# Thin-head attention with its value products gathered from two key blocks, a full last feed-forward block, and stored parts without repetition

## The chip, the cores and the metric

The kernel runs on one core of one Trainium2 chip. The time is the device time of one execution in microseconds. Three executions of the kernel before took 7369.84 to 7376.01 us, median 7372.24 us.

## What is computed

The reference is a stack of four layers on 4096 rows of 256 features. Each layer is an attention-like part and a feed-forward-like part, and each part ends in a residual addition and a layer norm:

```
x = _layernorm(x + _L0_attn_ref(...))   # 16 heads of 16 features, causal, rotary
x = _layernorm(x + _L0_ffn_ref(...))    # two local transformers; each ends in a gated feed-forward, 682 hidden
x = _layernorm(x + _L1_attn_ref(...))   # 16 heads of 16, relative-position bias, not causal
x = _layernorm(x + _L1_ffn_ref(...))    # projection with quantised operands
x = ...                                 # L2: state scan, experts; L3: recurrence
x = _layernorm(x + _L3_ffn_ref(...))    # two local transformers again
```

The change touches the two thin-head attentions (L0 and L1), the four gated feed-forwards, and the output projection of the L1 attention.

## The kernel before, in words

The stack is a sequence of stages with a barrier between them. The names of tiles begin with the stage: Aqkv, Aatt, Aout for the L0 attention; B0ffn and B1ffn, later H0ffn and H1ffn, for the gated feed-forwards; Cqkv, Catt, Cout for the L1 attention; Dmx is the stage after it.

**Products for the heads (`stage_qkv`, L584 to L733).** There are 8 chunks of 512 rows (B = 4 batches, two halves). In a chunk TensorE makes four product blocks (Q and K, two halves of the features each) and then four blocks of V. VectorE turns each Q or K block into an f32 tile, casts it to bf16 (the first of three parts) and subtracts (`split_high`, L660); GpSimd makes the second and third part. ScalarE's queue issues the stores. Q and K are stored as a stack of six terms in `q_parts` and `k_parts`, in which parts are repeated (Q: 0,1,2,0,1,0; K: 0,0,0,1,1,2), so that a score is a sum over 96 rows. The tile of parts and the tile of V have two buffers each; a buffer is free again when its stores have landed (`o_out`, `vo_out`).

**Thin attention (`stage_thin_attention`, L1077 to L1460).** Work goes over 8 pairs of heads times 4 batches; this gives 32 rounds of 16 steps. The order on each engine is written out by `written_out` (L101): at step i TensorE runs `scores` of step i (1024 keys for 128 queries; causal: only those up to the query), `turn_maxima`, `scores_by_key` of unit i-26 (two halves of 512 queries, called c = 0 and 1) and `values` of unit i-29. VectorE runs `add_near` of unit i-26 (Catt alone: it adds the near part of the bias to the queries close to the key block), and then `mask` of step i, which also takes the row maximum. ScalarE runs the exponentials of unit i-26, c = 0 before c = 1, and further on `move_out`, which copies the finished output of a round. Unit i of a round is head i % 2 of key block i // 2; the `values` call of unit i multiplies V with the half c = i % 2 of both heads of its key block, on four strips of 32 columns of the array.

The scores of a step have a ring of two buffers (`s_ps`), so that `scores` of step i waits for `mask` of step i-2. The products by key have a ring of two banks in Catt and three in Aatt (`T_R`), so in Catt a half c of a unit waits for the exponential of the same half of the unit before it. The output has one bank in Aatt, two in Catt (`O_R`). The exponentials' tile holds four key blocks (`NB`).

**Gated feed-forward (`stage_gated_ffn`, L1697).** The hidden 682 features are 5 blocks of 128 and one of 42. `down` (L1868) accumulates for each 128 rows the products of the six blocks (L1876). An f32 matmul is two instructions in the trace.

**Output projection (`stage_thin_out`, `Tail`).** `Tail` adds the residual, normalises and stores the result by rows; it also transposes it on TensorE (`turn`, L253), copies it on ScalarE and stores it by columns.

Of the kernel before, what the change touches and what calls it, by code (L numbers as in the profile page):

```python
# [16 lines left out]
ALU = mybir.AluOpType  # L17
# [9 lines left out]
B = 4  # L27
# [14 lines left out]
Q_STACK = ((0, 3, 0), (3, 2, 0), (5, 1, 0))  # L42
K_STACK = ((0, 3, 0), (3, 2, 1), (5, 1, 2))
# [99 lines left out]
class Tail:  # L143
# [4 lines left out]
    def __init__(self, nc, pl, out, res, base=None, bias=None, norm=True, y_ring=2, t_ring=2, tp=None, final=None):  # L148
        self.nc, self.pl, self.out, self.res, self.base, self.bias, self.norm = nc, pl, out, res, base, bias, norm
        self.y_ring, self.t_ring, self.final = y_ring, t_ring, final  # L150
# [18 lines left out]
        if final is None:  # L169
# [32 lines left out]
    def combine(self, v, it, u):  # L202
# [27 lines left out]
        for g in range(LN):  # L230
            m = u - (LN - 1) + g
            if self.final is None:
                v.wait_ge(self.t_done, it * NT + (m + 1))
# [9 lines left out]
    def prime_pe(self, t):  # L243
        t.sem_inc(self.y_done, NT)
        t.wait_ge(self.ident_made, 1)
        if self.final is None:
            t.sem_inc(self.t_done, LN)
# [5 lines left out]
    def turn(self, t, it, u):  # L253
        if self.final is not None:
            return
# [9 lines left out]
    def prime_act(self, s):  # L265
        if self.final is None:
# [3 lines left out]
        for i in range(IN if self.final is None else 0):  # L270
            s.sem_inc(self.cols_out[i], 16)

    def store(self, s, it, u):
# [5 lines left out]
        s.dma_start(rows_of(self.out, it, u * P, P), self.xn[:, g, :]).then_inc(self.rows_out[g], 16)  # L279
        s.wait_ge(self.t_done, n + 1 + LN)  # L280
# [6 lines left out]
    def finish(self, s):  # L287
# [3 lines left out]
        for i in range(IN if self.final is None else 0):  # L291
# [292 lines left out]
def stage_qkv(nc, name, act_in, wq, wk, wv, wqs, wks, bias, rope, q_s, k_s, v_s, scale):  # L584
# [5 lines left out]
    with ExitStack() as ctx:  # L590
# [16 lines left out]
        o_out = [pl.sem(f"o_out{i}") for i in range(2)]  # L607
# [52 lines left out]
        def split_high(v, s, it, c, j):  # L660

            v.drain()
            v.wait_ge(o_out[s], it * 192 + (c * 2 + j // 2 + 1) * 48)
            v.tensor_copy(parts[:, s, 0, :], o_sb[:, s, :])
            v.drain()
            v.tensor_tensor(rest[:, s, :], o_sb[:, s, :], parts[:, s, 0, :], ALU.subtract).then_inc(o_high, 1)

        @block.gpsimd
        def _(g):
            g.sem_inc(o_used, 2)  # L670
            with g.Fori(0, B) as it:
                for i in range(8):
# [3 lines left out]
                    g.tensor_copy(parts[:, s, 1, :], rest[:, s, :])  # L676
                    g.drain()
                    g.tensor_tensor(parts[:, s, 2, :], rest[:, s, :], parts[:, s, 1, :], ALU.subtract).then_inc(o_used, 1)
# [3 lines left out]
        def _(v):  # L682
# [3 lines left out]
            for it in range(B):  # L686
                for c in range(2):
# [16 lines left out]
                    for u in range(4):  # L704
                        s, n = u % 2, it * NT + (c * 4 + u)
                        v.wait_ge(v_done, n + 1 + NT)
                        v.wait_ge(vo_out[s], it * 64 + (c * 2 + u // 2 + 1) * 16)
                        if roped:
                            v.tensor_tensor(vo[:, s, :], v_ps[s][:], brow[:], ALU.add).then_inc(vo_done, 1)
# [2403 lines left out]
```

## Time and profile before

| | us |
|---|---|
| median of three executions | 7372.24 |
| profiled execution, its own time | 7380.4 |
| its span, first to last instruction | 7378.7 |
| TensorE busy | 6109.4 (83%) |
| VectorE busy | 4644.4 (63%) |
| ScalarE busy | 2720.1 (37%) |
| GpSimd busy | 1321.6 (18%) |
| mean granted TensorE clock | 0.921 of full |

The profile is one execution. Busy shares are averages over many stages with different limits, so each stage is read in its own stretch of time: Aqkv begins at 98.6 us, Aatt has its first score at 306.0 us, Cqkv begins at 2703.6 us, Catt has its first score at 2885.8 us, and Cout runs until about 3955 us.

### The profile page before, as it was taken

What the parts mean: (1) busy time and instruction counts of PE and PEld (TensorE: products, weight loads), DVE (VectorE), ACT (ScalarE), POOL (GpSimd) and SP (SyncE); (2) the same over time, 40 slices, a digit from 0 to 9 for tenths busy, and PEclk for the clock granted to TensorE, in tenths of its full rate; (3) what the DMA queues carried; (4) which work ended last, traced back from release to release, by engine and by line L of the source; (5) the groups of instructions that cost most, each with busy time, mean ns of one, the idle gap of its engine ahead of it and who ended that gap; (6) DMA issues with size and microseconds to landing.
All of it is one profiled execution on the core that took longest, in us unless ns stands there. A gap on an engine that the chain in (4) does not pass through costs nothing. (4 is left out here: it accounts for less than half of the span.)

```text
span 7378.7 us, 109245 instructions
## 1 busy us (share of the span) xinstructions
PE 6109.4 (83%) x31152; PEld 3249.8 (44%) x31152; DVE 4644.4 (63%) x11759; ACT 2720.1 (37%) x6050; POOL 1321.6 (18%) x1051
## 2 busy tenths in 40 slices
PE   5788859989988976999974488987996888998989
PEld 2333334655456542222223353334554456444755
DVE  4666648634764546999967648984435775347735
ACT  0155514722364211666651115541110354224711
POOL 1211107100431012000000005540002431015100
PEclk9899979989999987999997799988998999999989
DMA  5433244662456435323314221124222456224641
GB/s 163 134 70 72 64 126 146 199 201 72 133 177 203 136 109 161 89 73 88 87 48 117 82 75 48 37 61 112 69 67 86 133 168 216 73 90 152 195 147 54
DMA packets 946481, 836.62 MB, mean 113 GB/s; under 512 B 240872, under 2 KB 801984, under 8 KB 945728
## 3 DMA queue, kind: packets, MB, share of 16 engines
q1 hardware_dynamic: 498352, 507.29, 23.9%
q10 hardware_dynamic: 425472, 304.20, 13.3%
q0 software_dynamic: 22144, 18.99, 0.8%
q8 instruction: 236, 3.87, 0.2%
q14 instruction: 277, 2.27, 0.1%
HBM read 506.25 MB, written 346.03 MB: 116 GB/s over the span
## 5 line engine op out<-in xcount | busy, mean ns | idle before, releaser
L1414 ACT ACTIVATE Catt_E<-Catt_t 128x512 f32<-128x512 f32 x1024 | 579.2, 596 | 320.5 <-DVE Catt_t L1377 242.1
L1363 DVE CUSTOM_DVE_ANT_0 Catt_S<-Catt_s,Catt_win 128x1024 f32<-128x1024 f32 x512 | 621.5, 1215 | 5.8 <-DMA Catt_win<-skewed 3.9
L1363 DVE CUSTOM_DVE_ANT_0 Aatt_S<-Aatt_s,Aatt_win 128x128 f32<-128x128 f32 (+7 forms) x512 | 379.1, 757 | 227.9 <-PE Aatt_s L1290 201.1
L1414 ACT ACTIVATE Aatt_E<-Aatt_t 128x512 f32<-128x512 f32 (+3 forms) x768 | 341.4, 491 | 244.8 <-PE Aatt_t L1322 199.0
L1319 PE MATMUL Catt_t<-Catt_Q,Catt_K 123*128 123x512 bf16 x1024 | 363.8, 387 | 48.2 <-ACT Catt_E L1414 20.9
L1290 PE MATMUL Catt_s<-Catt_K,Catt_Q 96*128 96x512 bf16 x1024 | 321.9, 397 | 23.3 <-DMA Catt_K<-k_parts 12.3
L1377 DVE TENSOR_TENSOR Catt_t<-Catt_t,Catt_near 128x256 f32<-128x256 f32 (+2 forms) x640 | 284.7, 457 | 85.2 <-PE Catt_t L1319 77.1
L1341 PE MATMUL Catt_o<-Catt_E,Catt_V 128*32 128x256 f32 x4096 | 326.5, 391 | 0.0
L2381 PE MATMUL scan_cum<-scan_X,scan_upto 128*128 128x512 f32 x512 | 265.4, 608 | 25.8 <-DVE scan_X L2450 24.0
L2379 PE MATMUL scan_cum<-scan_X,scan_after 128*128 128x512 f32 x448 | 239.6, 617 | 40.8 <-DVE scan_pi L2461 40.8
L1341 PE MATMUL Aatt_o<-Aatt_E,Aatt_V 128*32 128x256 f32 (+1 forms) x2816 | 220.7, 358 | 41.6 <-ACT Aatt_O L1422 41.6
L1290 PE MATMUL Aatt_s<-Aatt_K,Aatt_Q 96*128 96x512 bf16 (+3 forms) x768 | 220.0, 343 | 38.2 <-DVE Aatt_nmax L1363 26.7
L1319 PEld LDWEIGHTS Catt_t<-Catt_Q,Catt_K 123*128 123x128 bf16 x1024 | 96.2, 96 | 342.7 <-ACT Catt_E L1414 297.4
L1319 PE MATMUL Aatt_t<-Aatt_Q,Aatt_K 99*128 99x512 bf16 (+3 forms) x768 | 232.2, 333 | 14.9 <-ACT Aatt_turned L1404 11.5
L2648 ACT ACTIVATE moe_sg<-moe_g 128x512 f32<-128x512 f32 x80 | 47.8, 597 | 361.4 <-PE moe_u L2591 361.4
L2381 PEld LDWEIGHTS scan_cum<-scan_X,scan_upto 128*128 128x128 f32 x512 | 99.6, 196 | 155.7 <-issue 155.7
L1290 PEld LDWEIGHTS Catt_s<-Catt_K,Catt_Q 96*128 96x128 bf16 x1024 | 58.9, 98 | 245.8 <-DVE Catt_nmax L1363 118.6
L2591 PE MATMUL moe_g<-moe_xc,moe_wg 128*128 128x512 f32 x320 | 154.8, 607 | 11.9 <-DVE moe_hid L2724 11.6
L2362 POOL TENSOR_TENSOR scan_pr<-scan_pr,scan_pi 128x1024 f32<-128x1024 f32 x64 | 150.9, 2358 | 42.4 <-DVE scan_pr L2461 42.4
L2379 PEld LDWEIGHTS scan_cum<-scan_X,scan_after 128*128 128x128 f32 x448 | 83.4, 195 | 166.2 <-issue 166.2
L2355 POOL TENSOR_TENSOR scan_X<-scan_cs,scan_r 128x1024 f32<-128x1024 f32 x64 | 121.7, 1902 | 188.8 <-DVE scan_X L2450 188.8
L2167 PE MATMUL state_in_z<-state_in_wj,state_in_xc 128*128 128x288 f32 x512 | 140.8, 431 | 15.9 <-DVE state_in_wj L2192 15.9
(723 smaller groups left out, 14037.1 us busy)
## 6 DMA issues: line engine op xcount, KB each, us to landing
moe_cb<-c_s SPq DMA_DIRECT2D x16, 1024.0 KB
skewed<-lines POOLq DMA_DIRECT2D x8, 1920.0 KB, 12.8
Catt_win<-skewed SPq DMA_DIRECT2D x16, 960.0 KB, 4.8
rec<-state_in_r ACTq DMA_DIRECT2D x32, 416.0 KB
scan_r<-rec SPq DMA_DIRECT2D x64, 208.0 KB, 2.5
Aatt_Q<-q_parts SPq DMA_DIRECT2D x32, 384.0 KB, 4.2
Aatt_K<-k_parts SPq DMA_DIRECT2D x32, 384.0 KB, 5.5
Catt_Q<-q_parts SPq DMA_DIRECT2D x32, 384.0 KB, 4.3
```

The costliest lines, as they stand in the source:

```text
L1290: ins = t.matmul(s_ps[j % 2][:, c:d], Q[0:K0, b, h, u * P:(u + 1) * P], K[0:K0, b, h, c:d], start=True, stop=True)
L1319: ins = t.matmul(bank(it, n)[:, 0:hi - lo], K[:, b, h, kb * P:(kb + 1) * P], Q[:, b, h, lo:hi], start=True, stop=not diagonal)
L1341: ins = t.matmul(o_ps[b % O_R][f:f + 2 * hd, k0 * P:k1 * P], V[:, b, kb, h, :], blocks[:, h, x, k0:k1, :], start=kb == 0 and c == 0, stop= ...
L1363: v.tensor_tensor_reduce(out=S[:, j % 2, 0:w], in0=s_ps[j % 2][:, 0:w], in1=win[:, 0 if causal else h, w0:w0 + w], scale=-1.0, scalar=BIG, ...
L1377: v.tensor_tensor(x, x, near[:, b, h, a - (kb - 1) * P:z - (kb - 1) * P], ALU.add).then_inc(near_done, 1)
L1414: a.activation(E[:, kb % NB, h, lo:hi], bank(it, n)[:, 0:hi - lo], ACT.Exp, scale=scale).then_inc(exped, 1)
L2167: t.matmul(z_ps[s][:], xc[:, c, kt, q * P + j + 1:q * P + j + 1 + P], wj[:, kt, j, :], start=j == 0 and kt == 0, stop=j == TAPS - 1 and kt ...
L2355: g.tensor_tensor(X[:, m % 4, 0, :].rearrange("p (k e) -> p k e", k=16), cs[:, m % 2, :].rearrange("p (k e) -> p k e", k=16), r[:, m % R, ...
L2362: g.tensor_tensor(pr[:, m % 2, :], pr[:, m % 2, :], pi[:, m % 2, :], ALU.add).then_inc(sum_done, 1)
L2379: t.matmul(cum[i][:, c:c + 512], after[:], X[:, (j - 1) % 4, i, c:c + 512], start=False, stop=False, skip_group_check=True)
L2381: ins = t.matmul(cum[i][:, c:c + 512], upto[:], X[:, j % 4, i, c:c + 512], start=u == 0, stop=True, skip_group_check=True)
L2591: ins = t.matmul(ps[k % 2][:], w[:, kt, j * P:(j + 1) * P], xc[:, c, kt, :], start=kt == 0, stop=kt == KT - 1)
```

## The change

The diff has five parts.

1. In both thin attentions the value products are no longer made at each step. They are made for four units (two key blocks) in a row, at the step at which the last of them was made before.
2. `q_parts` and `k_parts` hold each of the three parts once, not six terms. Each product block is stored by three DMAs of one part each; the loads of the attention make the stack: three DMAs for Q and six for K in place of one and one. The tile of parts has four buffers, and V has one per half; a chunk's V is stored by one DMA in place of four.
3. In the gated feed-forward the last block is used in full: rows 42 to 127 of `hid` and `w2_sb` are set to zero once by GpSimd, and the product goes over 128 rows.
4. The Cout stage no longer makes the transposed result (`cols=False`): no transposes, no ScalarE copies, no stores by columns.
5. Waits are counted to match; VectorE waits for the zeroed tails once, and the sync queue before its last weight load.

```diff
-Q_STACK = ((0, 3, 0), (3, 2, 0), (5, 1, 0))
-K_STACK = ((0, 3, 0), (3, 2, 1), (5, 1, 2))
+STACK = ((0, 3, 0), (3, 2, 1), (5, 1, 2))
...
     def turn(self, t, it, u):
-        if self.final is not None:
+        if not self.cols:
             return
...
         s.dma_start(rows_of(self.out, it, u * P, P), self.xn[:, g, :]).then_inc(self.rows_out[g], 16)
+        if not self.cols:
+            return
...
+        PR = 4
-        parts = pl.sb("parts", [P, 2, PARTS, CH], BF16)
+        parts = pl.sb("parts", [P, PR, PARTS, CH], BF16)
-        vo = pl.sb("vo", [P, 2, C])
+        vo = pl.sb("vo", [P, 2, 4, C])
...
-            v.wait_ge(o_out[s], it * 192 + (c * 2 + j // 2 + 1) * 48)
-            v.tensor_copy(parts[:, s, 0, :], o_sb[:, s, :])
+            v.wait_ge(o_out[j], it * (32 * PARTS) + (c + 1) * (16 * PARTS))
+            v.tensor_copy(parts[:, j, 0, :], o_sb[:, s, :])
...
-                        v.wait_ge(vo_out[s], it * 64 + (c * 2 + u // 2 + 1) * 16)
+                        if u == 0:
+                            v.wait_ge(vo_out[c], it * 16 + 16)
...
-                        for t0, nt, part in K_STACK if w else Q_STACK:
-                            a.dma_start((k_s if w else q_s)[m * P:(m + 1) * P, t0:t0 + nt, bass.ds(it * T + c * CH, CH)],
-                                        parts[:, s, part:part + 1, :].to_broadcast([P, nt, CH]) if w else
-                                        parts[:, s, part:part + nt, :]).then_inc(o_out[s], 16)
-                    for u in range(4):
-                        s, n = u % 2, it * NT + (c * 4 + u)
-                        a.wait_ge(vo_done, n + 3)
-                        a.dma_start(v_s[bass.ds(it * T + (c * CH + u * P), P), 0:C], vo[:, s, :]).then_inc(vo_out[s], 16)
+                        rows = (k_s if w else q_s).rearrange("(e k f) t -> e k f t", k=PARTS, f=16)[m * 8:(m + 1) * 8, :, :, bass.ds(it * T + c * CH, CH)]
+                        for k in range(PARTS):
+                            a.dma_start(rows[:, k], parts[:, j, k, :]).then_inc(o_out[j], 16)
+                    a.wait_ge(vo_done, it * NT + (c * 4 + 6))
+                    a.dma_start(v_s[bass.ds(it * T + c * CH, CH), 0:C].rearrange("(q p) d -> p q d", p=P), vo[:, c]).then_inc(vo_out[c], 16)
...
-                for x, x_s in ((Q, q_s), (K, k_s)):
-                    sp.dma_start(x[0:K0, b], x_s.rearrange("f t c -> (f t) c")[bass.ds(it * (2 * K0), 2 * K0), b * T:(b + 1) * T]
-                                 .rearrange("(h p) c -> p h c", h=2)).then_inc(head_in[b], 16)
+                for t0, nt, part in STACK:
+                    rows = slice(t0 * hd, (t0 + nt) * hd)
+                    sp.dma_start(Q[rows, b], head_rows(q_s, it, b)[:, 0:nt * hd].rearrange("h p c -> p h c")).then_inc(head_in[b], 16)
+                    for h in range(2):
+                        sp.dma_start(K[rows, b, h], head_rows(k_s, it, b)[h:h + 1, part * hd:(part + 1) * hd].to_broadcast([nt, hd, T])
+                                     ).then_inc(head_in[b], 16)
...
-            written_out(t, PAIRS, ST, ((0, scores), (TURN, turn_maxima), (LAG, scores_by_key), (LAG + 3, values)))
+            def values_of_two_blocks(it, i):
+
+                if i % 4 == 3:
+                    for k in range(i - 3, i + 1):
+                        values(it, k)
+
+            written_out(t, PAIRS, ST, ((0, scores), (TURN, turn_maxima), (LAG, scores_by_key), (LAG + 3, values_of_two_blocks)))
...
+            g.memset(hid[:, :, NJ - 1, :], 0.0).then_inc(tails_zero, 1)
+            g.memset(w2_sb[:, NJ - 1, :], 0.0).then_inc(tails_zero, 1)
...
-                        ins = t.matmul(tail.y[u % 2][:], hid[0:M[j], c, j, (u % 4) * P:(u % 4 + 1) * P], w2_sb[0:M[j], j, :],
+                        ins = t.matmul(tail.y[u % 2][:], hid[:, c, j, (u % 4) * P:(u % 4 + 1) * P], w2_sb[:, j, :],
...
-    stage_thin_out(nc, "Cout", oT_s, i["L1_wo"], nxt, cur)
+    stage_thin_out(nc, "Cout", oT_s, i["L1_wo"], nxt, cur, cols=False)
```

## Rows read from the trace of the kernel before

**Rows 1.** Windows: stretch, its us, busy of each engine, granted clock, DMA share, GB/s.

```profile
338.00:922.00 584.00, 512.38 (x4592) 200.93 (x4591) 363.42 (x989) 343.33 (x780) 61.64 (x149) 0.99 0.30 67
1600.00:1868.00 268.00, 264.06 (x849) 145.97 (x848) 103.44 (x306) 65.28 (x136) 8.61 (x8) 0.99 0.32 95
2707.00:2876.00 169.00, 109.24 (x253) 59.82 (x251) 76.50 (x127) 0.00 (x0) 57.04 (x64) 0.81 0.58 191
2932.00:3792.00 860.00, 820.50 (x5796) 222.97 (x5799) 803.42 (x1592) 563.82 (x1021) 61.87 (x149) 1.00 0.31 78
```

**Rows 2.** Lines by form, Catt on VectorE: busy, mean ns | idle before, releasers.

```profile
L1363 DVE CUSTOM_DVE_ANT_0 Catt_S<-Catt_s,Catt_win 128x1024 f32<-128x1024 f32 x512 | 621.5, 1215 | 5.8 <-DMA Catt_win<-skewed 3.9 <-issue 0.5
L1377 DVE TENSOR_TENSOR Catt_t<-Catt_t,Catt_near 128x384 f32<-128x384 f32 x256 | 145.1, 567 | 55.8 <-PE Catt_t L1319 52.3
L1377 DVE TENSOR_TENSOR Catt_t<-Catt_t,Catt_near 128x256 f32<-128x256 f32 x256 | 110.1, 430 | 19.0 <-PE Catt_t L1319 15.3
```

**Rows 3.** Source line L1363 from 3000 to 3700 us: min/median/max ns, first and last start.

```profile
L1363 DVE CUSTOM_DVE_ANT_0 Catt_S<-Catt_s,Catt_win x391: 1210/1215/1225, 3000.5 to 3699.3; 128x1024 f32<-128x1024 f32 x196
```

**Rows 4.** Timeline of TensorE in Catt: start, us, instruction, count.

```profile
3351.71 0.64 PE L1341 MATMUL Catt_o<-Catt_E,Catt_V 128*32 128x256 f32 x8
3352.28 0.60 PE L1290 MATMUL Catt_s<-Catt_K,Catt_Q 96*128 96x512 bf16 x2
3352.73 0.60 PE L1319 MATMUL Catt_t<-Catt_Q,Catt_K 123*128 123x512 bf16 x2
3353.26 0.64 PE L1341 MATMUL Catt_o<-Catt_E,Catt_V 128*32 128x256 f32 x8
```

**Rows 5.** Timeline of VectorE and ScalarE in Catt, single rows.

```profile
3356.65 0.57 DVE L1377 TENSOR_TENSOR Catt_t<-Catt_t,Catt_near 128x384 f32<-128x384 f32 x1 [0.25 <-PE Catt_t L1319]
...
3358.33 0.57 DVE L1377 TENSOR_TENSOR Catt_t<-Catt_t,Catt_near 128x384 f32<-128x384 f32 x1
...
3357.25 1.08 ACT L1414 ACTIVATE Catt_E<-Catt_t 128x512 f32<-128x512 f32 x2 [0.86 <-DVE Catt_t L1377]
```

**Rows 6.** Timeline of TensorE at the end of Catt: four units in a row.

```profile
3838.38 1.93 PE L1341 MATMUL Catt_o<-Catt_E,Catt_V 128*32 128x256 f32 x32
```

**Rows 7.** Timeline in B0ffn: the products of `down`, and the weight loads of the short block.

```profile
1625.20 11.89 PE L1876 MATMUL B0ffn_y<-B0ffn_w,B0ffn_hid 128*128 128x256 f32 x48
...
1627.45 0.29 PEld L1876 LDWEIGHTS B0ffn_y<-B0ffn_w,B0ffn_hid 42*128 42x128 f32 x2 [0.33 <-issue]
```

**Rows 8.** Aatt: the masks of all rounds (tile Aatt_s), and TensorE's timeline.

```profile
L1363 DVE CUSTOM_DVE_ANT_0 Aatt_S<-Aatt_s,Aatt_win x512: 285/756/1226, 309.3 to 923.5; 128x768 f32<-128x768 f32 x22, 128x128 f32<-128x128 f32 x22, 128x512 f32<-128x512 f32 x22, 128x640 f32<-128x640 f32 x21
...
610.63 0.64 PE L1341 MATMUL Aatt_o<-Aatt_E,Aatt_V 128*32 128x256 f32 x8 [1.34 <-ACT Aatt_O L1422]
```

**Rows 9.** Waits in Cqkv (us, times, longest), and one chunk's end in the timeline.

```profile
DVE Cqkv_vo L711 <- DMA v_s<-Cqkv_vo: 59.6, 12, 8.7
DVE Cqkv_parts L664 <- DMA q_parts<-Cqkv_parts: 27.6, 15, 3.5
...
2763.86 3.78 PE L656 MATMUL Cqkv_v<-Cqkv_w_v,Cqkv_hT 128*128 128x256 f32 x8 [6.23 <-DVE Cqkv_vo L711]
2767.44 3.65 PE L650 MATMUL Cqkv_a<-Cqkv_hT,Cqkv_w_q 128*128 128x512 f32 x8
...
2772.51 0.68 DVE L693 TENSOR_SCALAR Cqkv_o<-Cqkv_a 128x512 f32<-128x512 f32 x1
```

**Rows 10.** The same place in Aqkv.

```profile
126.11 1.88 PE L650 MATMUL Aqkv_b<-Aqkv_hT,Aqkv_w_qs 128*128 128x512 f32 x4
...
128.36 0.74 DVE L697 SCALAR_TENSOR_TENSOR Aqkv_tmp<-Aqkv_a,Aqkv_bcol,Aqkv_cos 128x512 f32<-128x512 f32 x1
```

**Rows 11.** Timeline of VectorE in Cout: a wait for TensorE.

```profile
3877.57 0.42 DVE L208 TENSOR_TENSOR Cout_z<-Cout_y,Cout_res 128x256 f32<-128x256 f32 x1 [0.41 <-PE Cout_y L1502]
```

**Rows 12.** DMA: ScalarE's queue from 2707 to 2876 us; a load, median us to landing.

```profile
q10 hardware_dynamic: 30432, 29.11, 51.5%
...
Catt_K<-k_parts SPq DMA_DIRECT2D x31, 384.0 KB, 5.7
```

More of the change, by code:

```diff
@@ L143, with __init__ @@
 class Tail:
-    def __init__(self, nc, pl, out, res, base=None, bias=None, norm=True, y_ring=2, t_ring=2, tp=None, final=None):
+    def __init__(self, nc, pl, out, res, base=None, bias=None, norm=True, y_ring=2, t_ring=2, tp=None, final=None, cols=True):
         self.nc, self.pl, self.out, self.res, self.base, self.bias, self.norm = nc, pl, out, res, base, bias, norm
-        self.y_ring, self.t_ring, self.final = y_ring, t_ring, final
+        self.y_ring, self.t_ring, self.final, self.cols = y_ring, t_ring, final, cols and final is None
         self.y = [pl.ps(f"y{i}", (P, C)) for i in range(y_ring)]
@@ L269, in prime_act @@
             s.sem_inc(self.rows_out[i], 16)
-        for i in range(IN if self.final is None else 0):
+        for i in range(IN if self.cols else 0):
             s.sem_inc(self.cols_out[i], 16)
@@ L290, in finish @@
             s.wait_ge(self.rows_out[i], 16 + 16 * B * NT // LN)
-        for i in range(IN if self.final is None else 0):
+        for i in range(IN if self.cols else 0):
             s.wait_ge(self.cols_out[i], 16 + 16 * B * NT // IN)
@@ L662, in split_high @@
             v.drain()
-            v.wait_ge(o_out[s], it * 192 + (c * 2 + j // 2 + 1) * 48)
-            v.tensor_copy(parts[:, s, 0, :], o_sb[:, s, :])
+            v.wait_ge(o_out[j], it * (32 * PARTS) + (c + 1) * (16 * PARTS))
+            v.tensor_copy(parts[:, j, 0, :], o_sb[:, s, :])
             v.drain()
-            v.tensor_tensor(rest[:, s, :], o_sb[:, s, :], parts[:, s, 0, :], ALU.subtract).then_inc(o_high, 1)
+            v.tensor_tensor(rest[:, s, :], o_sb[:, s, :], parts[:, j, 0, :], ALU.subtract).then_inc(o_high, 1)
         @block.gpsimd
@@ L675, in _ @@
                     apart(g, pl.pool_unread)
-                    g.tensor_copy(parts[:, s, 1, :], rest[:, s, :])
+                    g.tensor_copy(parts[:, i % PR, 1, :], rest[:, s, :])
                     g.drain()
-                    g.tensor_tensor(parts[:, s, 2, :], rest[:, s, :], parts[:, s, 1, :], ALU.subtract).then_inc(o_used, 1)
+                    g.tensor_tensor(parts[:, i % PR, 2, :], rest[:, s, :], parts[:, i % PR, 1, :], ALU.subtract).then_inc(o_used, 1)
                     g.drain()
@@ L1460, in _, with stage_thin_out @@
                 a.wait_ge(o_out[i], 64 + 64 * PAIRS)
-def stage_thin_out(nc, name, oT_s, w, out, res, bias=None):
+def stage_thin_out(nc, name, oT_s, w, out, res, bias=None, cols=True):
     with ExitStack() as ctx:
         pl = Pool_(nc, ctx, name)
-        tail = Tail(nc, pl, out, res, None, bias, True)
+        tail = Tail(nc, pl, out, res, None, bias, True, cols=cols)
         w_sb = pl.sb("w", [P, KT, C])
@@ L1719, in stage_gated_ffn @@
         a_ps = [pl.ps(f"a{i}") for i in range(2)]
-        small_in, wl_zero, w1_in, w2_in = (pl.sem(n) for n in ("small_in", "wl_zero", "w1_in", "w2_in"))
+        small_in, wl_zero, w1_in, w2_in, tails_zero = (pl.sem(n) for n in ("small_in", "wl_zero", "w1_in", "w2_in", "tails_zero"))
         hs_in = [pl.sem(f"hs_in{i}") for i in range(LN)]
@@ L1827, in _ @@
             v.wait_ge(small_in, 64)
+            v.wait_ge(tails_zero, 2)
             batches(v, batch)
```

32 lines of the change are left out of this document (18 added, 14 removed).

## The prediction

> **What bounds the kernel now.** I read the windows by stage first, because the page's mean (TensorE 83% busy) mixes stages with different limits. Then came, for each stage that the change touches, the lines, the waits and the timeline of the engine that is never idle there.
>
> Catt: TensorE is busy 820 of 860 us and VectorE 803 of 860 [rows 1]; both look full. The timeline separates them. A step of TensorE is products by key to values 0.53 us, values to scores 0.57, scores to products by key 0.45, together 1.55 us [rows 4]. VectorE needs 1.68 us for a step with a near part of 384 queries (start to start in [rows 5]), and by the mean durations [rows 2] 1.54 with 256 and 1.82 where the near part falls in both halves. Of a round's 16 units 4 have 256, 8 have 384 and 4 have both: 4 x 1.54 + 8 x 1.68 + 4 x 1.82 = 26.9 us. The round really takes 16 x (3699.3 - 3000.5)/390 = 28.7 us [rows 3]. So VectorE bounds Catt, and 1.8 us a round are its waits for products by key [rows 2, 5]. Aatt has no near part; VectorE is busy 62%, TensorE 88% [rows 1], and a round takes 16 x (923.5 - 309.3)/511 = 19.2 us [rows 8]: TensorE bounds it. In the feed-forward TensorE is busy 264 of 268 us [rows 1]. In Cqkv VectorE stands 59.6 + 27.6 = 87 of 169 us before buffers whose stores have not landed [rows 9].
>
> **Feed-forward.** Four row blocks of 12 matmuls take 11.89 us [rows 7]. In an unbroken run such matmuls start every 0.22 us: 32 of them, four side by side, take 1.93 us, the last 0.38 of it [rows 6]. With 47 such intervals and the last matmul that is 10.3 + 0.4 = 10.7, so 1.2 us less; the rest sits at the loads of the 42-row block, each behind 0.33 us [rows 7], and the exit from the last block adds 0.1 to 0.2. I take 0.36 us a row block, 32 blocks, 4 stages: -46 us (bounds -38 and -52). All of it is on the path, since nothing else is as busy. The two memsets run beside the first weight loads; VectorE's wait stands ahead of its first gate, with the combines behind it, and the sync queue's ahead of the last weight load and the residual loads, none of which is wanted for tens of us. Uncovered they cost 1 to 2 us a stage.
>
> **Cqkv.** V now has a buffer for each of a chunk's four blocks, so the waits of 59.6 us go; the parts have four buffers, so the 27.6 us go. Late next is TensorE: the third and fourth V block start when VectorE has freed the first two (2763.86), and the next chunk's first Q block follows at 2767.44 and is ready half of 3.65 us later, 2769.3; VectorE began it at 2772.51 [rows 9]. That gives 3.2 us a chunk, and the parts another 2.5: 5.7 x 8 = -45 us. Bounds: -87 if all waits go, -10 if the longer store of V and GpSimd's parts, which VectorE must share time with, take their place. In Aqkv the same change meets a later TensorE: the second product of the next chunk ends at 126.11 + 1.88 = 127.99, and VectorE started at 128.36 [rows 10]. That is 0.4 x 8 = 3, with the end -4 us (0 to -20, if the clock stays high there).
>
> Here a rule of the Trainium skill bears on the cost. "DMA: Bandwidth & Descriptors", section "Why a DMA increments its semaphore by 16 and not by 1", says that a DMA is spread over the largest number up to 16 that divides both sides' slowest dimension. The new stores of parts have 8 there, so by it they use half the engines. No trace here shows it. In rows: ScalarE's queue took 51.5% of 16 x 169 us for 30432 packets, 0.046 us each [rows 12]. A chunk now has 12 stores of 128 packets, on 8 engines 12 x 16 x 0.046 = 8.8 us, and V 1.5, under a chunk of about 15 us. So by itself it does not bind, but it is the reason why I give the loss of this gain a chance.
>
> **Cout.** The transposes stand between TensorE's products; VectorE waits 0.41 us [rows 11] and some 0.2 more for them in each group of four row blocks. 0.6 x 8 and the last copy and store by columns: -6 us (0 to -10).
>
> **The loads.** Nine DMAs stand where two stood, 7 more at about 0.45 us of issue, 3 us a load, with V, tables, window and the round trip of the maxima queued behind them. A load starts when the round's values are done, 20 steps before its first score, 24 us in Aatt and 35 in Catt; before, it landed 5.7 us after issue [rows 12]. Hidden but for the first load of each stage: +5 us for both (0 to +10). Without that cover it would be 3 us a round.
>
> **Values in Catt.** A unit in a run costs 0.43 us (1.93 less 0.64, over three [rows 4, 6]), alone it costs 0.53 + 0.57 less 0.44 (products by key to scores directly): 0.66. Merging saves TensorE 0.23 x 12 = 2.8 us a round, but TensorE is not the bound. What counts is where the run stands. At every fourth step TensorE does: products by key of unit k, then 0.53, then the run of four until the next scores 0.57 + 1.29 = 1.86, then 0.45 of scores, and only then the products by key of unit k+1, 2.84 us after those of unit k. It cannot make them earlier: the engine works in order, and the ring of two banks makes them wait for the exponentials of unit k. VectorE's near part of unit k+1 waits for them, and the next mask is queued behind it, though its scores are there. Where the near part is in the first half, the second half of unit k is held back by its exponential: near part 0.57, two exponentials 1.08 [rows 5] and hand-over, 1.75 us after the near part of unit k-1 against a step of 1.68. With a product's 0.42 until VectorE may start, the run then begins 0.27 later: 3.1 us. So the round's four steps with a run cost 2 x 2.84 + 2 x 3.1 = 11.9 us. The other twelve go at VectorE's pace, since TensorE has 0.9 us of work in them: 3 x 1.54 + 6 x 1.68 + 3 x 1.82 = 20.2. With 0.4 for the turned maxima the round is 32.5 us instead of 28.7: +3.8 x 32 = **+122 us**. Bounds: +150 if all four steps lose another 0.2, and -75 if the order did not hold VectorE and its waits for products by key went altogether (55.8 + 19.0 [rows 2]); I take 122, because each of its terms is a row.
>
> **Values in Aatt.** 12 runs a round become 4, 8 x 0.2 = 1.6 us less. The first values of a round now come three steps later, and so the wait of 1.34 us for the one output bank [rows 8] goes, since ScalarE's copy has long been made. 2.9 us on offer. Against it: in the twelve steps without values TensorE runs into VectorE's masks (up to 1.2 us each for 1024 keys [rows 8]) and ScalarE's exponentials (two in 0.99, being 1.08 less 0.09 of hand-over [rows 5]). Walking the round with these, I lose half: -1.4 x 32 = -45 us (bounds 0 and -93). The exponentials' buffers are free in time: unit k waits for the values of unit k-8, made at least two steps before.
>
> **Sum.** -46 - 45 - 4 - 6 + 5 - 45 + 122 = -19 us. The profiled execution took 7380.4 (span 7378.7), 8 above the median; the sum holds for either: 7361 for such a profile, **7353 us** for the median. About 0.2%, 15 us, is what a measurement of this kernel tells from no change.
>
> **Rivals.**
> Runs do not stall VectorE in Catt, and its waits shrink. For it: TensorE is 95% busy there and VectorE does wait for it. Against: the order on both engines. Half to all of the 75 us gained instead of 122 lost: 7153 to 7195, say 7185.
> The granted clock falls in Catt. It is 1.00 at 95% busy, but 0.81 in Cqkv at 65% [rows 1]; with runs I expect (0.95 x 28.7 - 2.8)/32.5 = 75% busy. At 0.90, a fifth of the time at 1.2 GHz, a step with a run grows by some 2.4 us: 4 x 0.2 x 2.4 = 1.9 a round, +61: 7414, slower than before. Against: the gaps are 1.3 us at most, in Cqkv 6.23 [rows 9]. It decides the sign from about 0.94.
> The stores pay nothing in Cqkv (fewer engines, or GpSimd takes the waits over): +45, 7398, slower.
> The change does not do what it says, in that the 42-row block is no dearer than a full one: +46, 7399. The 0.33 us before its loads speak against it; I count it with the one before.
>
> **How the numbers follow.** Forecast 0.60, with its own range 7315 to 7390; first rival 0.14, second 0.13, third with fourth 0.13. The forecast's terms err by some 30 us together, mostly Catt and Aatt, so within it faster, same, slower are 0.58, 0.28, 0.14. That gives faster 0.35 + 0.14 + 0.01 = 0.50, slower 0.08 + 0.12 + 0.09 = 0.29, the same 0.21. The range leaves out most of the first rival and little above: 7265 to 7420.
>
> **What would show it.** In Catt, four steps of a round at 2.8 to 3.1 us between masks, the idle time of L1377 before products by key up from 75 to about 200 us, TensorE's share down, clock still 1.00. In Aatt no wait for the output copy and rounds near 17.8 us. In the feed-forward 48 matmuls in 10.6 us. In Cqkv chunks of 15 us and no DMA wait. Wrong it would be if Catt's rounds stayed under 29 us, or if its clock fell.

## The result, and the profile after

The kernel after takes 7492.72 us (median of 4 runs, 7483.19 to 7503.07), the kernel before beside it 7374.12 (7369.84 to 7385.87): ratio 1.0159, 95% interval 1.014 to 1.0177, 119 us slower where 19 us faster was forecast, and outside the range. The profiled execution is the shortest of the four, 7483.19 us with a span of 7481.5, 103 above the span of before; the stages below add up to that.

From the end of the stage before to its own end, each stage changed by (us, after less before; a stage ends with the last operation of TensorE, VectorE or ScalarE on its tiles): Aqkv -12.9, Aatt +4.2, the four feed-forwards -10.6, -12.3, -12.5, -12.9, Cqkv -38.0, Catt **+193.6**, Cout -5.0, the stage behind it -2.4; the others, whose code is the same, together +12 (in the traces of the experiments these lie between -3 and +15, so that is scatter). One stage turns the sign.

The windows of the kernel after, in the order of [rows 1] (us, busy of PE, PEld, DVE, ACT, POOL, granted clock, DMA share, GB/s):

```profile
325.00:912.00 587.00, 498.26 (x4606) 227.33 (x4604) 355.56 (x996) 339.79 (x786) 61.66 (x149) 0.98 0.29 67
1582.00:1849.00 267.00, 252.18 (x855) 151.97 (x856) 108.44 (x330) 67.37 (x141) 8.63 (x8) 0.97 0.34 103
2680.00:2809.00 129.00, 100.72 (x248) 57.37 (x246) 84.61 (x124) 0.00 (x0) 57.80 (x64) 0.82 0.48 148
2860.00:3922.00 1062.00, 858.39 (x5908) 287.36 (x5908) 828.70 (x1634) 569.16 (x1052) 62.81 (x153) 0.94 0.24 64
```

In Catt TensorE and VectorE were 95% and 93% busy; now they are 81% and 78% busy. Neither is full, so they wait for each other. VectorE's lines there, as [rows 2], and its masks over the same part of the stage as [rows 3]:

```profile
L1377 DVE CUSTOM_DVE_ANT_0 Catt_S<-Catt_s,Catt_win 128x1024 f32<-128x1024 f32 x493 | 598.3, 1214 | 0.5
L1391 DVE TENSOR_TENSOR Catt_t<-Catt_t,Catt_near 128x384 f32<-128x384 f32 x248 | 140.5, 566 | 127.6 <-PE Catt_t L1327 127.6
L1391 DVE TENSOR_TENSOR Catt_t<-Catt_t,Catt_near 128x256 f32<-128x256 f32 x246 | 105.9, 430 | 101.4 <-PE Catt_t L1327 99.6
```

```profile
L1377 DVE CUSTOM_DVE_ANT_0 Catt_S<-Catt_s,Catt_win x376: 1211/1214/1225, 3001.1 to 3799.7; 128x1024 f32<-128x1024 f32 x188
```

The operations cost what they did. The idle time before the near parts went from 75 to 229 us, and a round takes 16 x 798.6/375 = 34.1 us. Where a round loses it is seen in TensorE's and ScalarE's timelines, as [rows 4, 5]:

```profile
3244.58 1.93 PE L1349 MATMUL Catt_o<-Catt_E,Catt_V 128*32 128x256 f32 x32
3246.45 0.60 PE L1298 MATMUL Catt_s<-Catt_K,Catt_Q 96*128 96x512 bf16 x2
...
3248.56 0.88 PE L1327 MATMUL Catt_t<-Catt_Q,Catt_K 123*128 123x512 bf16 x2 [0.64 <-ACT Catt_E L1428]
3249.28 0.60 PE L1298 MATMUL Catt_s<-Catt_K,Catt_Q 96*128 96x512 bf16 x2
3250.86 0.88 PE L1327 MATMUL Catt_t<-Catt_Q,Catt_K 123*128 123x512 bf16 x2 [0.99 <-ACT Catt_E L1428]
3251.58 0.87 PE L1298 MATMUL Catt_s<-Catt_K,Catt_Q 96*128 96x512 bf16 x2
3252.55 1.09 PE L1327 MATMUL Catt_t<-Catt_Q,Catt_K 123*128 123x512 bf16 x2
3253.57 2.70 PE L1349 MATMUL Catt_o<-Catt_E,Catt_V 128*32 128x256 f32 x32
...
3248.88 0.60 ACT L1436 ACTIVATE Catt_O<-Catt_o 128x512 f32<-128x512 f32 x1
3249.57 0.54 ACTq L1439 DMA_DIRECT2D Catt_sums<-Catt_O  x1
3250.21 1.09 ACT L1428 ACTIVATE Catt_E<-Catt_t 128x512 f32<-128x512 f32 x2 [0.73 <-DVE Catt_t L1391]
```

A run of 32 products takes 1.93 us, as in [rows 6]. Two gaps of TensorE follow the round's last run, with different causes. The first, 0.64 us, ends at 3248.56, before ScalarE begins its copy: it is the run's own, through VectorE's late near part and the exponential behind it. The second, 0.99 us, is that of exponentials that stand behind ScalarE's output copy and the issue of a DMA, 1.14 us together. Then the granted clock falls, and the next run takes 2.70. The same place in windows (their columns as above):

```profile
3238.30:3251.90 13.60, 10.51 (x70) 3.42 (x62) 10.31 (x22) 7.12 (x14) 1.27 (x1) 1.00 0.17 55
3251.90:3255.30 3.40, 3.31 (x24) 1.06 (x26) 2.95 (x6) 2.16 (x4) 0.83 (x4) 0.52 0.71 99
```

In Aatt [rows 8] the wait of 1.34 us for the output bank is gone, and this stands in its place in every round:

```profile
578.25 0.60 ACT L1436 ACTIVATE Aatt_O<-Aatt_o 128x512 f32<-128x512 f32 x1
...
578.93 0.54 ACTq L1439 DMA_DIRECT2D Aatt_sums<-Aatt_O  x1
...
579.58 1.81 ACT L1428 ACTIVATE Aatt_E<-Aatt_t 128x256 f32<-128x256 f32 x5 [0.73 <-ACT Aatt_O L1436]
...
580.02 0.39 PE L1327 MATMUL Aatt_t<-Aatt_Q,Aatt_K 99*128 99x512 bf16 x1 [1.26 <-ACT Aatt_E L1428]
```

Waits (us, times, longest) at the head of Catt, and in Cqkv, where [rows 9] had 59.6 and 27.6 us for DMAs and now no DMA stands among VectorE's waits. Of the 12.4 us for windows 3.8 lie ahead of the stage's first mask and 8.6 ahead of the ninth. Then the products of [rows 7], whose 48 starts now span 10.1 us:

```profile
PE Catt_s L1298 <- DMA Catt_K<-k_parts: 15.0, 1, 15.0
DVE Catt_S L1377 <- DMA Catt_win<-skewed: 12.4, 2, 8.6
...
DVE Cqkv_vo L714 <- PE Cqkv_v L658: 22.2, 15, 1.8
DVE Cqkv_o L695 <- PE Cqkv_a L652: 16.1, 7, 2.5
```

```profile
L1894 PE MATMUL B0ffn_y<-B0ffn_w,B0ffn_hid x48: 379/379/379, 1616.1 to 1626.2; 128*128 128x256 f32 x48
```

### The profile page after: what moved, and what is told of

It is laid out like the page before. It is cut to its first block and busy times, and to the rows that moved or that the text cites. A ratio compares the mean times of both kernels' runs of the same rounds, so it can differ in the third digit from the quotient of the medians.

```text
span 7481.5 us, 109988 instructions
## 1 busy us (share of the span) xinstructions
PE 6055.3 (81%) x31088; PEld 3357.7 (45%) x31088; DVE 4646.3 (62%) x11759; ACT 2688.4 (36%) x6018; POOL 1328.2 (18%) x1059
## 5 line engine op out<-in xcount | busy, mean ns | idle before, releaser
L1377 DVE CUSTOM_DVE_ANT_0 Catt_S<-Catt_s,Catt_win 128x1024 f32<-128x1024 f32 x512 | 620.8, 1214 | 14.0 <-DMA Catt_win<-skewed 12.4
L1327 PE MATMUL Catt_t<-Catt_Q,Catt_K 123*128 123x512 bf16 x1024 | 385.4, 406 | 184.5 <-ACT Catt_E L1428 147.4
L1349 PE MATMUL Catt_o<-Catt_E,Catt_V 128*32 128x256 f32 x4096 | 282.9, 423 | 0.0
L1349 PEld LDWEIGHTS Catt_o<-Catt_E,Catt_V 128*32 128x32 f32 x4096 | 130.1, 120 | 130.1 <-issue 68.8
L1349 PE MATMUL Aatt_o<-Aatt_E,Aatt_V 128*32 128x256 f32 (+1 forms) x2816 | 178.5, 367 | 0.0
L1281 POOL TENSOR_TENSOR Catt_O<-Catt_O,Catt_Rb 128x512 f32<-128x512 f32 x32 | 40.8, 1274 | 723.0 <-DMA Catt_Rb<-r_s 723.0
L1298 PEld LDWEIGHTS Catt_s<-Catt_K,Catt_Q 96*128 96x128 bf16 x1024 | 77.2, 99 | 197.4 <-DVE Catt_nmax L1377 110.2
```

The source lines that it names most:

```text
L1298: ins = t.matmul(s_ps[j % 2][:, c:d], Q[0:K0, b, h, u * P:(u + 1) * P], K[0:K0, b, h, c:d], start=True, stop=True)
L1327: ins = t.matmul(bank(it, n)[:, 0:hi - lo], K[:, b, h, kb * P:(kb + 1) * P], Q[:, b, h, lo:hi], start=True, stop=not diagonal)
L1349: ins = t.matmul(o_ps[b % O_R][f:f + 2 * hd, k0 * P:k1 * P], V[:, b, kb, h, :], blocks[:, h, x, k0:k1, :], start=kb == 0 and c == 0, stop= ...
L1377: v.tensor_tensor_reduce(out=S[:, j % 2, 0:w], in0=s_ps[j % 2][:, 0:w], in1=win[:, 0 if causal else h, w0:w0 + w], scale=-1.0, scalar=BIG, ...
```

## The experiments

The stages are apart from one another, so one kernel can carry an edit in each. Step k is the time from a round's mask k to the next mask; a round is 16 steps. This table is worked out from VectorE's timeline of each trace: mean rounds from the third on (us), medians of the steps that matter, and how often the granted clock falls from 2.4 to 1.2 GHz in the stage. Where the text speaks of rounds without a fall, they are counted from step 8 to step 8, since most falls lie near a round's end.

```
                 Catt round  steps 0 / 4 / 8 / 12 / 14 / 15          falls  Aatt round  falls
before             28.67     1.68  1.68  1.55  1.68  2.17  1.90         0     19.47       3
after              34.12     3.60  2.84  2.84  3.11  2.30  2.12        30     19.45       7
e1 step by step    28.73     1.68  1.68  1.55  1.68  2.17  1.90         0     19.58       5
e2 runs alone      34.14     3.61  2.84  2.84  3.11  2.30  2.12        31     19.54       8
e3 PE kept busy    34.21     2.95  2.84  2.84  3.54  2.30  1.90        12     18.25       0
e4 two units       30.68     2.09  1.97  1.97  2.24  2.30  1.90         2     18.63       0
e5 third bank      31.46     2.76  2.84  2.45  2.69  1.61  1.67        14     17.92       0
e6 first run only  27.32     2.76  1.61  1.47  1.61  1.61  1.67         0     18.13       0
e7 bank, loads     29.17     1.67  1.61  1.47  1.61  2.45  1.67        16     18.73       5
e8                 27.34     2.76  1.61  1.47  1.61  1.61  1.67         0     17.82       0
e9 shorter runs    28.18     1.67  1.61  1.47  1.61  1.61  3.02         7     18.59       2
e10 two banks      30.62     3.95  1.68  1.55  1.68  2.30  2.12        25     19.81       6
e11 issue later    34.07     2.95  4.38  2.84  3.11  1.68  1.90        28     18.76       0
```

**e1, step by step again in both attentions.**

```
-            written_out(t, ..., (LAG + 3, values_of_two_blocks)))
+            written_out(t, ..., (LAG + 3, values)))
```

> The kernel after, with the value products of both attentions issued step by step again; the other three parts of the change stay. Theory 1 (the runs of four are what costs: in Catt VectorE starves behind each run, in Aatt they are worth nearly nothing): Catt's rounds go back from 34.1 to 28.7 us, 31 x 5.4 = 170 us, Aatt's stay at 19.3; the whole is about 7295 us, 75 to 80 us below the kernel before. Theory 2 (the nine loads of parts per batch in place of two, and their 5 to 9 us of landing, hold up the rounds of Catt): rounds stay above 31 us and the whole above 7370.

Measured: 7312.38 us (7310.96 to 7314.04), 0.9908 of the kernel before (0.9891 to 0.9924). The runs are the whole loss; the rest of the change is worth 70 us. Catt, with the loads of the kernel after and rounds as before, is 10.0 us longer than in the kernel before: that is what the loads cost there. VectorE's waits for products by key fall back:

```profile
DVE Catt_t L1391 <- PE Catt_t L1327: 50.8, 143, 1.4
```

**e2, the runs alone on the kernel before.** The diff is `values_of_two_blocks` and its place in the order, nothing else.

> The kernel before with nothing changed but the value products in runs of two key blocks. Theory 1: Catt's rounds are 33.5 to 34.2 us as in the kernel after, so the whole is 160 to 180 us over the kernel before, 7535 to 7555 us, and Catt's first mask starts where it did. Theory 2 (the loads of parts and the runs cost together): rounds near 31 us, the whole under 7470.

Measured: 7562.05 us (7559.54 to 7571.73), 1.025 (1.0232 to 1.0267), +179. The same steps to 0.01 us, with two loads in place of nine: the loads have no part in the rounds.

```profile
DVE Catt_t L1383 <- PE Catt_t L1319: 210.8, 203, 2.8
```

**e3, three edits.**

```
+                again = 2 if not causal and j % GS in (13, 14, 15) else 1     # (a) scores
-                for c in range(0, w, CH):
+                for c in list(range(0, w, CH)) * again:
...
-            ..., (LAG + 4, move_out), ...        # (b) copy and issue of sums in one
+            ..., (LAG + 4, move_out), (LAG + (6 if causal else 4), gather_sums), ...
...
+                        rows = P if j < NJ - 1 else 64 if base is not None else 96     # (c)
-                        ... hid[:, c, j, ...], w2_sb[:, j, :], ...
+                        ... hid[0:rows, c, j, ...], w2_sb[0:rows, j, :], ...
```

> The kernel after with three separate edits. (a) Catt: the score products of steps 13 to 15 of each round are issued twice, 0.43 us each, in time in which TensorE now idles 1.0 to 1.4 us. If its idling there is what the granted clock answers to, the clock no longer falls at the run of step 0, step 0 goes from 3.6 to 3.1 us and the round from 34.1 to 33.5 (18 us in all); if the fall has another cause, the round stays or grows by up to 1.3 us. (b) Aatt: ScalarE's issue of the sums' DMA stands two steps behind the output copy instead of right behind it. If the 0.54 us of issue are the half of step 15 that matters, step 15 goes from 2.13 to about 1.6 us and the round from 19.05 to 18.5; if the copy alone sets it, nothing moves. (c) Feed-forward: the last hidden block of the down products has 96 rows in B0 and H0 and 64 in B1 and H1 instead of 128. If the 42-row block was dear because its weight load is not taken ahead at a size other than 128 rows, all four stages are 10 to 13 us longer than in the kernel after; if only sizes under some bound are dear, 96 rows cost nothing.

Measured: 7477.72 us (one run). (a) No fall at steps 14 and 15 any more (25 of 30 before), step 0 down from 3.60 to 2.95; but 8 of the 12 falls that are left are at step 3, and step 12 pays 0.43 us for the doubled scores. The mean round doesn't gain; the 17 rounds without a fall take 33.6 us. (b) Aatt's round falls by 1.2 us, and TensorE's wait ahead of its products by key from 1.26 to 0.43 us: the issue was in the way. Part of the 1.2 is the clock, which no longer falls; rounds without a fall went from 19.13 to 18.25. (c) The block of 96 rows runs like a full one (48 starts in 10.1 us), the one of 64 (11.6) like that of 42 in [rows 7] (11.5), with the same 0.33 us before its loads. That is the second reading, only sizes under some bound are dear; the bound lies between 64 and 96 rows.

```profile
L1901 PE MATMUL B0ffn_y<-B0ffn_w,B0ffn_hid x48: 377/379/381, 1587.7 to 1597.8; 128*128 128x256 f32 x40, 96*128 96x256 f32 x8
...
L1901 PE MATMUL B1ffn_y<-B1ffn_w,B1ffn_hid x48: 376/379/483, 2386.3 to 2397.9; 128*128 128x256 f32 x40, 64*128 64x256 f32 x8
...
2388.59 0.29 PEld L1901 LDWEIGHTS B1ffn_y<-B1ffn_w,B1ffn_hid 64*128 64x128 f32 x2 [0.33 <-issue]
```

**e4, runs of two units.** `if i % 2 == 1: for k in (i - 1, i)`; in Aatt `move_out` at LAG + 5. The condition on `i` holds in both attentions, so Aatt has runs of two as well, and not of four as the expectation says.

> The kernel after with (a) Catt: runs of two units (one key block, 16 products, 0.96 us) instead of four; Theory 1 (VectorE starves for what of a run does not fit under the bank that it has in hand): a run of two adds 0.2 to 0.5 us at eight steps, the round is 30 to 32 us, 34.1 with four and 28.7 with one; rival (any run costs a fixed stall of about 1.2 us, whatever its length, by a refilled pipeline or the clock): 8 x 1.2 more than 28.7, 38 us. (b) Aatt: runs of four as in the kernel after, but ScalarE's output copy and sums issue one step later. If the copy stands in the way because it waits for the last run, step 15 goes from 2.1 to below 1.7 us and the round to about 18.5; if it is the 1.14 us of ScalarE's own time, the loss moves one step on and the round stays at 19.05.

Measured: 7332.71 us, 0.9935 (0.9914 to 0.9955). Catt 30.68, as the theory of what doesn't fit under the bank in hand has it; a fixed stall per run is excluded. Its eight run steps take 1.83 to 2.30. Aatt tests nothing about the copy alone, since its runs are shorter too. Its steps 14 and 15 together take 3.93 us against 2.88 in the kernel after, and the wait for the output bank is back in every round; steps 0, 4 and 12 are shorter by 2.1, and the clock no longer falls:

```profile
575.77 1.07 PE L1349 MATMUL Aatt_o<-Aatt_E,Aatt_V 128*32 128x256 f32 x16 [1.35 <-ACT Aatt_O L1436]
```

**e5, a third bank for products by key in Catt.**

```
-        T_R, O_R = (3, 1) if causal else (2, 2)
+        T_R, O_R = 3, 1
```

In Aatt the output copy is `v.tensor_copy` on VectorE at LAG + 4, the sums' issue on ScalarE at LAG + 6; `window(0, 1)` stands behind `window(0, 0)`; the value blocks of `stage_qkv` are stored one by one.

> The kernel after with (a) Catt: three banks for the products by key and one for the values in place of two and two, the runs of four units kept. Theory 1 (with two banks VectorE has nothing in hand behind a run) says that a third lets it work on by one unit: the four run steps lose 0.5 to 1.1 us each and the round goes from 34.1 to 30 to 32 us. Rival (the run's 1.9 us of TensorE has to be paid anyway, because TensorE is busy 0.81 of the time and catches up late): the round stays above 33. The clock's falls at steps 14 and 15 stay in both. (b) Aatt: the copy of the output bank made by VectorE and the issue of the sums' DMA two steps later: if ScalarE's copy is worth anything beside the issue, the round goes below the 18.25 us that the later issue alone gave, to about 17.7; if not, it stays. (c) Cqkv: the value blocks are stored one by one as before, the parts unrepeated as after: if the stores of parts carry the gain, the stage is 145 to 148 us from end to end as in the kernel after; if the values' single store does, it is over 160. (d) The second window of Catt is loaded right behind the first: the 9.8 us in which VectorE waits for it in the first batch go.

Measured: 7318.46 us (one run). (a) 31.46, inside the forecast; but the gain isn't at all runs: step 4 is unchanged at 2.84 and 8 of 14 falls come just ahead of it. (b) 17.92. (c) Cqkv 145.1 us from end to end, 145.5 in the kernel after: the single store of V has no share in the gain. The eight V buffers stayed, so what they and the four buffers of parts each carry was not tried. (d) VectorE's waits for windows are gone; the second of them was 8.6 us.

**e6, only the first four units of a round in a run.**

```
-                if i % 4 == 3:
+                if i % GS >= 4:
+                    values(it, i)
+                elif i % GS == 3:
                     for k in range(i - 3, i + 1):
                         values(it, k)
```

with three banks and one in Catt, and the issue two steps later in Aatt.

> The kernel after with, in both attentions, a run only for the first four units of a round (so that the first value products come after the output bank is free) and the rest step by step; three banks for products by key and one for values in Catt; the issue of the sums' DMA two steps later in Aatt. Theory 1: a run costs where it stands, so Catt pays one and not four, 28.7 plus 0.5 to 1.3 us a round; Aatt keeps the relief at its bank and loses the stalls of steps 4 and 12, 17.6 to 18.0 us a round against 18.25. Whole: 7235 to 7285 us. Rival: the fourth run matters because the granted clock falls anywhere that TensorE idles, rounds of Catt over 31.

Measured: 7207.59 us, 0.9766 (0.9716 to 0.9816), below the forecast. Catt's round is 27.32 where 29.2 to 30 was expected, and its clock never falls. I had priced the run and not what the third bank gives to the other steps: 1.61 in place of 1.68, 1.61 and 1.67 at steps 14 and 15. The 26.9 us of the prediction is thus not VectorE's own pace. Its steps without a wait are 1.48 and 1.61 us here, 0.06 to 0.07 less than those that 26.9 was added up from; with them (4 x 1.48 + 8 x 1.61 + 3 x 1.67 + 1.81, the last four where the near part falls in both halves) I estimate VectorE's own round at 25.6.

```profile
L1379 DVE CUSTOM_DVE_ANT_0 Catt_S<-Catt_s,Catt_win x512: 1211/1215/1225, 2782.6 to 3653.6; 128x1024 f32<-128x1024 f32 x171
```

**e7, the third bank without any run in Catt; K's first loads on ScalarE.** Aatt as e6, issue at LAG + 7.

> The kernel after with (a) Catt step by step, three banks and one: if the depth of the ring limits Catt even without runs, its round goes below 28.7 (to 27.5), but the values must now wait for the single output bank, up to 1.2 us a round; my estimate is 28 to 29.5. (b) Aatt: first run only, the sums' DMA three steps later: 17.6 to 18.0 us a round as with two steps. (c) The first six loads of K parts of each attention are issued by ScalarE instead of SyncE, which takes 0.9 to 1.6 us over each pair, and the second window comes early: the first mask of Catt comes 3 to 6 us earlier, if issue and not the transfer is what it waits for. Whole: 7225 to 7270 us.

Measured: 7278.4 us, 0.9862 (0.9815 to 0.9908), 8 above the forecast's end. (a) 29.17: with a single output bank the values stand before ScalarE's copy every round, step 13 takes 3.67, and in 16 of the rounds the clock falls there. (c) A miss: the first mask comes 21.9 us after Cqkv's end, not sooner than 16.8. But ScalarE issued its six loads from 4.9 to 10.0 us after Cqkv's end, and SyncE's last load of K in the kernel after is issued by 9.8: the issue did not come earlier, and both windows and V were now loaded beside it. So what these loads wait for stays open.

```profile
PE Catt_o L1351 <- ACT Catt_O L1444: 63.7, 29, 2.2
```

```profile
PE Catt_s L1300 <- DMA Catt_K<-k_parts: 21.0, 1, 21.0
```

**e8, what the others point to:** e6 with e5's copy on VectorE and early window.

> First run only in both attentions, three banks and one in Catt (27.3 us a round so far), the second window early, and in Aatt VectorE's copy of the output bank with the sums' issue two steps later. If the gains in Aatt of the copy on VectorE (17.92 against 18.25 us with all runs) and of the first run only (18.13 with ScalarE's copy) are separate, Aatt's round is 17.3 to 17.8 us; Catt's stays at 27.3 and starts its rounds 8 us sooner after its first mask. Whole: 7180 to 7195 us. If the clock takes part of it back in Aatt (falls while TensorE waits), its round stays above 18.1.

Measured: 7191.21 us (7187.86 to 7192.77), **0.9734** of the kernel before (0.9721 to 0.9748), 194 us faster, and 301 below the kernel after. Both attentions run at a full clock:

```profile
330.00:850.00 520.00, 484.87 (x4454) 205.39 (x4453) 364.73 (x992) 315.37 (x733) 59.35 (x144) 1.00 0.32 75
2820.00:3630.00 810.00, 747.34 (x5708) 231.89 (x5707) 763.88 (x1570) 545.87 (x1006) 60.80 (x148) 1.00 0.32 83
```

The two gains in Aatt don't add up: 17.82 us against 17.92 with all four runs.

**e9, the run at the head shorter,** three units in Catt and two in Aatt.

> As the last, but the run at the head of a round has three units in Catt and two in Aatt. A run of four costs step 0 of Catt 2.76 us against 1.67; with three units TensorE's run is 0.5 us shorter and one step earlier. Theory 1: Catt's round falls by 0.3 to 0.6 us to 26.7 to 27.0, and Aatt's by 0 to 0.4. Rival: the output bank isn't free yet when the shorter run comes (ScalarE copies it in step 13 or 14), and the wait for it costs what the run gives back: Catt's round 27.3 or more, and with TensorE idle the clock falls.

Measured: 7239.56 us, 0.9801 (0.9783 to 0.9819). The rival: step 0 gives back 1.1 us, step 15 takes 1.35 more, and the clock falls 7 times. Of the lengths tried, four units is the one at which the output bank is free.

**e10, the single run with two banks and two in Catt;** in Aatt step by step, with the issue two steps later.

> (a) Catt: a run only for the first four units, with the banks as in the kernel after, two and two. It parts the third bank from the single run. Theory 1: 28.7 of the step-by-step order plus 1.2 to 1.9 us of the one run with its clock fall, 29.9 to 30.6 us a round; then the third bank is worth some 2.5 us a round beside it. Rival (the single run alone explains the 27.3 us): below 28.7. (b) Aatt: values step by step, with the sums' issue two steps later. The 1.3 us wait for the output bank stays and ScalarE's issue is hidden, as before: 19.2 to 19.4 us a round; if it falls towards 18.2, the issue was what cost before as well, and the runs nothing.

Measured: 7375.47 us (one run). Catt 30.62, so against e6 the third bank (with one for the values in place of two) is worth 3.3 us a round, 1.2 of it at step 0 (3.95 against 2.76), ahead of which the clock falls in 24 rounds here and in none of e6. The three rounds that no fall touches take 29.5, so some 2.2 us are the bank's own and the rest comes through the clock. Aatt 19.81: without runs the late issue is worth nothing, since the wait at the bank stays.

**e11, the sums' issue two steps later in Catt, the kernel after otherwise;** in Aatt the copy on VectorE, the issue right behind.

> The kernel after with (a) Catt: ScalarE's issue of the sums' DMA two steps behind its copy of the output bank instead of right behind it. In the kernel after the copy takes 0.60 us and the issue 0.54 us ahead of a unit's exponentials, steps 14 and 15 take 2.30 and 2.12 us, TensorE idles 0.64 and 0.99 us in them, and the granted clock falls in 25 of 30 cases in just these two. If the issue behind the copy is the cause of both, the two steps lose 0.3 to 0.6 us, the falls at steps 14 and 15 go, step 0 goes from 3.6 to 3.1, and the round from 34.1 to 33.0 to 33.4 us. If the copy or the bank of two is the cause, the round stays above 33.8. (b) Aatt: the copy is made by VectorE, with ScalarE's issue still right behind it in time, one step of the order later than the last run. If only the issue's place counts, ScalarE now waits for VectorE's copy as well and the round stays at 19 us or more; if ScalarE's 0.60 us for the copy count, it falls by up to 0.6.

Measured: 7444.8 us (one run). Steps 14 and 15 lose 0.84 us and step 0 loses 0.65, as the first theory says; the round stays at 34.07. Of the two gaps behind the last run the 0.64 us is still there, and the 0.99 has become 0.37. The fall of the clock has moved to step 3 in 25 of 28 cases, where TensorE waits for the turned maxima, and meets the run of step 4 instead:

```profile
3329.72 0.88 PE L1327 MATMUL Catt_t<-Catt_Q,Catt_K 123*128 123x512 bf16 x2 [0.64 <-ACT Catt_E L1436]
3331.40 0.88 PE L1327 MATMUL Catt_t<-Catt_Q,Catt_K 123*128 123x512 bf16 x2 [0.37 <-ACT Catt_E L1436]
...
3102.93 0.22 PE L1310 MATMUL Catt_t<-Catt_ident_b,Catt_parts 128*48 128x128 bf16 x1 [0.47 <-ACT Catt_E L1436]
3103.51 1.03 PE L1327 MATMUL Catt_t<-Catt_Q,Catt_K 123*128 123x512 bf16 x2 [0.36 <-ACT Catt_turned L1426]
3104.48 3.13 PE L1349 MATMUL Catt_o<-Catt_E,Catt_V 128*32 128x256 f32 x32
```

Without that fall the sum of its steps would be 34.07 - (4.38 - 2.84) = 32.5 us, and the two rounds without a fall take 32.5 and 32.9. The trace of the kernel after shows the same move by itself: in the five of its rounds that begin without a fall at steps 14 or 15 ahead of them, step 0 takes 2.9 us, and the clock falls at step 3 instead. In Aatt the copy's engine alone is worth 0.7 us a round, the issue's place alone 1.2 (e3), both 1.5 (e5); in all three the clock's 7 falls are gone too, which is part of it. Against the 19.13 us of the rounds without a fall in the kernel after, they are worth 0.4, 0.9 and 1.2.

## Why the prediction was wrong, by its own steps

The forecast was -19 us, the two traces differ by 103. Catt makes 69 of the difference (forecast +122 and half of +5, measured +193.6), Aatt 47 (-45 and the other half, measured +4.2), Cqkv 7.

**Values in Catt: the mechanism was right, the size was not.** The four steps were to take 2.84, 2.84 and twice 3.1; they take 2.84, 2.84, 3.11 and 3.60. Two terms of the walked round were mis-sized. "The other twelve go at VectorE's pace", 20.2 + 0.4: they take 34.0 - 12.4 = 21.6. The first is this one: the sum of VectorE's durations left out ScalarE's chain, its output copy and the issue behind it at steps 14 and 15, worth 0.84 us by e11. The second is the clock: I made it a rival of its own, at 0.90 and +61 us, instead of asking what the forecast's own gaps would do. A fall of the clock was one of the prediction's own signs of being wrong. It came to 0.94, where I had put the change of sign, but by itself it is only 29 x 0.65 = 19 us. Per round it is 0.65 us as it falls in the kernel after, and 1.5 us once the other loss is gone, so that taking away the 0.84 alone gained nothing. With neither, the round is the 32.5 us that the walk gave. The 1.68 us that the walk took for VectorE's own step holds with two banks only; e6 shows 1.61 with three, and what the other 0.07 are was not asked.

In numbers: 29 rounds x 5.45 = 158 us in place of 110, and 5 more in the last round; the drain from the last mask to VectorE's last operation 69.6 us in place of 49.0 (66.4 in e2, 49.0 in e1, so it is the runs'), which I hadn't priced: +21. The loads make the remaining 10. (A small slip beside it: the first rival's lower end adds up to 7156 us, not 7153.)

**The loads: +5 forecast, some +14 measured.** Entry of Aatt +3.9 us, of Catt +5.0 (first mask 16.8 us after Cqkv's end, was 11.7), and the second window, queued behind the eighteen loads of two batches, makes VectorE wait 8.6 us where it was 3.9: +4.7. The two in Catt are the 10.0 us that e1 shows there. "Hidden but for the first load of each stage" was right for the rest (e1, with rounds as before); what I missed is who stands last in SyncE's queue.

**Aatt: -45 forecast, 0 measured.** The wait at the bank went, and the step failed at "since ScalarE's copy has long been made". That step looked at the copy alone and not at what stands behind it on ScalarE. Copy and issue fall ahead of the next exponentials, and TensorE waits 1.26 us a round for these. e3, e5 and e11 show it: with the issue moved the round is 18.25, with the copy on VectorE as well 17.92. The forecast was 17.8 for the kernel without either edit, so that this number is close is luck.

**Right as forecast:** the feed-forward -48.3 (-46; 48 products in 10.5 us with the last one's 0.38), Cqkv -38.0 (-45), Cout with what follows -7 (-6). Aqkv gave -12.9 (-4, inside its bounds), between -6 and -14 in the kernels here that have the change; what sets it was not tried. The rival on Cqkv and the one on the 42-row block did not come true. The rule of the Trainium skill ("DMA: Bandwidth & Descriptors", section "Why a DMA increments its semaphore by 16 and not by 1"), by which a store with 8 at its slowest dimension uses half the engines, changes nothing in the time. 16390 packets took 38.7% of 16 x 129 us, 0.049 us each (0.046 before [rows 12]), and VectorE waits for no DMA; how many engines served them no run here shows.

## What to carry to other kernels

Group work only where the group fills a gap: a run at the one place where its output bank is busy anyway gains (27.32 us a round in e6 against 29.17 in e7), and the same run at three other places starves the engine that sets the pace (31.46 in e5). Before calling an engine full, look at its step where it waits for nothing. Before moving work away from a wait, look at what stands behind the copy that ended that wait, DMA issues included, for they are the next wait. And a gain at one place of a round can be taken back at another: where the clock fell once a round, closing one gap moved the fall to a later place.

## What the runs showed of the hardware

- The clock of TensorE does not follow from the size of one gap. Before, TensorE waited 0.32 us at step 14 and 0.36 us at the turned maxima in each round of Catt, and the clock never fell there. In the kernel after it went from 2.4 to 1.2 GHz behind gaps of 0.64 and 0.99 us, in e11 behind 0.47 and 0.36 with others of that size in the steps before, about once a round, and rose again during the run that followed. In e10 it fell in 24 rounds behind gaps of 0.37, 0.99 and 0.37 us. In e6 TensorE waits 0.28 and 0.98 us ahead of its run and 0.57 us at the maxima in every round, and it never falls; nor does it in e8, with nearly the same gaps. What parts these cases was not tried.

```profile
3326.07 0.39 PE L1327 MATMUL Catt_t<-Catt_Q,Catt_K 123*128 123x512 bf16 x1 [0.99 <-ACT Catt_E L1430]
```

- A weight load of 42 or 64 rows is not taken ahead (0.33 us of issue before it), one of 96 or 128 rows is. The load itself takes 0.185 us with 42 or 64 rows and 0.190 with 128. The Trainium skill, "TensorE: Matmul & The Clock Gate", section "Step-by-step: what each phase is for", says that the row count does not matter to a load's timing; the durations here agree. It also says that loads are pulled ahead where row groups don't conflict or where they go to the background buffer; the short blocks here are not pulled ahead, and which condition they miss no run shows.
- Six loads of K took ScalarE's queue 5.1 us to issue in e7, and the first score came 20.6 us after Cqkv's end, against 14.5 in the kernel after.
